# Attention with shared latents on one core: latents stationary in P.V, probabilities normalised before they are split

## The chip, the core and the metric

One Trainium2 chip, one of its cores. The kernel is one program of five engine queues: TensorE (PE), VectorE (DVE), ScalarE (ACT), GpSimd (POOL), and SyncE (SP), which issues all DMAs. The metric is the time of one execution on the device in microseconds, lower is better; the median of three executions is given.

## What is computed

A transformer layer on 2 x 1024 tokens of width 512. First latent attention with 32 heads, then a gated feed-forward part with whole-number weights. Only the attention is touched:

```python
q = (rms_norm(x @ wq_a.T) @ wq_b.T).reshape(b, s, 32, 128 + 64)      # rope on the last 64
kv = x @ wkv_a.T                                                     # 64 latents + 64 rope
kv_up = (rms_norm(kv_c) @ wkv_b.T).reshape(b, s, 32, 128 + 128)      # k_nope, v per head
scores = (q_nope @ k_nope.T + q_pe @ k_pe.T) * scale                 # causal mask
probs = softmax(scores)
out = (probs @ v) @ wo.T
x = x + layernorm(out)
```

The kernel never forms keys and values of a head. It folds the key weights into the query weights (`weff`), so that scores are queries against the 64 latents and 64 rotated columns that all heads share, and it folds each head's value weights with its part of `wo` (`m_fold`), so that P.V is probabilities times the 64 shared latents. Numbers that need more than one rounding are carried as a high and a low half.

## The kernel before

There are 64 heads (2 sequences x 32). A head has 8 query tiles of 128 tokens; tile j has (j + 1) x 128 keys, since later ones are masked. A pair of neighbouring tiles in the order `TILES` always has 9 key tiles together. For each tile i the steps are:

- PE `scores` (L1021): three matmuls for every stretch of up to 512 keys, into one of four PSUM slots `s_ps`, taken in turn. It waits for `split_low` of tile i - 4, the last reader of the slot.
- DVE `minimum` (L1453): adds the mask and takes the row minimum (scores are negated).
- ACT `exponential` (L1230), in place; then ACT `split_high` (L1238), probabilities times 2^15 rounded to f16; then DVE `split_low` (L1466), the rest, in f16.
- For two tiles together SP `turn_probs` (L822): one DMA transpose of both halves, from `pk` into `pt`.
- PE `values` (L1035): 18 matmuls, probabilities stationary, latents moving. The latents hold a high half, a low half and two columns of ones, 130 columns; the ones give the row sums.
- DVE `invert_sums` (L1462) reads the sums, ACT `outputs_norm` (L1247) scales the outputs into SBUF, twice a pair; POOL `outputs_add` (L1649) adds the two halves for four tiles.
- For two heads together PE `outputs_turn` (L1044) transposes four 128x128 tiles into the one bank `x_ps`, ACT `outputs_high` (L1256) and DVE `outputs_low` (L1473) split them.

Beside this runs `queries` for the next head (five matmuls into `x_ps`, ACT copy, two DMAs that swap rows, four POOL steps of rotation, POOL splits them into high and low), `fold_values` in the first 32 heads (into `x_ps` also), and for each group of four heads `output` (six matmuls a tile, `x_ps`) and `output_add` (DVE, L1489). Two PSUM banks are left beside the six of `s_ps`: `o_ps` and `x_ps`.

The order on every engine is fixed when the program is built. `attention_order` gives each step a place on a common scale, one unit to a tile (`at`, `then`), sorts them, and each engine runs its own steps in that order. Before, a step's distance from its tile is one number for all tiles. A place says only who comes before whom in one queue; when a step runs is decided by the semaphores it waits for.

Of the kernel before, what the change touches and what calls it, by code (L numbers as in the profile page):

```python
# [11 lines left out]
P = 128  # L12
# [23 lines left out]
NX, NA, NPK, NPT, NON = 4, 3, 3, 5, 8  # L36

SLOTS = (1, 2, 2, 1)
# [4 lines left out]
AFTER_SCORES = dict(minimum=0.8, exponential=1.24, split_high=2.06, split_low=2.28)  # L43
TURN_PROBS = 2.44
VALUES = 8.04
AFTER_VALUES = dict(invert_sums=1.21, outputs_norm=1.63, outputs_add=0.63)
TURN_STEPS = (6.26, 6.09)
AFTER_TURN = dict(outputs_high=0.27, outputs_low=0.95)
Q_STEPS = (0.84, 2.95)
AFTER_QUERIES = dict(queries_raw=0.13, queries_swap=0.31, queries_turn=0.13)  # L50
O_STEPS = (3.4, 6.23)
AFTER_OUTPUT = dict(output_add=1.26, output_store=1.5)
FOLD_STEP = 1.03
AFTER_FOLD = dict(fold_high=0.17, fold_low=1.03, fold_store=1.5)
# [24 lines left out]

LATW = P + 2  # L80
# [5 lines left out]
TILES = (3, 4, 6, 1, 2, 5, 7, 0)  # L86
# [15 lines left out]

def halves(j):

    width = (j + 1) * P
    return [(c, min(CW, width - c)) for c in range(0, width, CW)]
# [31 lines left out]
class Signals:  # L138


    def __init__(self, new):
# [67 lines left out]
def ot_count(n, c):  # L209

    return n // 2 * 2 + c + 1

# [57 lines left out]
class Memory:  # L270
    def __init__(self, whole, nc):
# [3 lines left out]
        with ExitStack() as attn:  # L275
# [5 lines left out]
            self.lat2 = sb(attn, "lat2", [P, NT, LATW], F16)  # L281
            sb(attn, "spare", [P, 2048 - NT * LATW // 2])
# [52 lines left out]
    def attention(self, ctx, sb, pb):  # L335
        self.m_in = sb(ctx, "m_in", [P, 2, GK, 2, DM], F32R)
        self.nbias = sb(ctx, "nbias", [P, 4])
        self.rinv = sb(ctx, "rinv", [P, NON])
        self.pk = sb(ctx, "pk", [P, NPK, 2 * PAIR, P], F16)
        self.pt = sb(ctx, "pt", [P, NPT, 2 * PAIR, P], F16)  # L340
        self.o_norm = sb(ctx, "o_norm", [P, NON, P])
        self.o_pair = sb(ctx, "o_pair", [P, 2, 4, P])
# [110 lines left out]
def attention_order(end):  # L453
# [1317 lines left out]
```

## Time and profile before

| | us |
|---|---|
| median of 3 runs | 1653.72 |
| lowest, highest | 1653.41, 1660.02 |
| profiled execution | 1654.97 |
| its span, first to last instruction | 1653.2 |

The profile is one execution. Its page gives busy times of the engines, the span in 40 slices, the DMA queues, the chain of work that ended last, and the costliest groups of instructions. Attention fills about the stretch from 100 to 1230 us, and its first 32 heads are those that also fold.

### The profile page before, as it was taken

The numbers are of one execution on the slowest core, as the hardware profiler recorded it, in microseconds if no ns is written. First come the engines' busy times: TensorE is split into PE (matmuls) and PEld (weight loads), VectorE is DVE, ScalarE is ACT, GpSimd is POOL, SyncE is SP. The second block draws the span as 40 slices with busy tenths as digits, with TensorE's granted clock in tenths as the row PEclk, the third lists the DMA queues.
The fourth block names the chain that finished last, engine by engine and source line by source line (L and its number), as shares of the span: only waits on it lengthen the run. The fifth ranks groups of instructions, "written<-read, shape, count | busy, mean of one in ns | idle before, by whom it ended". The sixth has DMA issues, their size and how long they took to land.

```text
span 1653.2 us, 30456 instructions
## 1 busy us (share of the span) xinstructions
PE 1552.6 (94%) x10720; PEld 1291.8 (78%) x10720; DVE 1113.6 (67%) x2509; ACT 1109.4 (67%) x2203; POOL 954.6 (58%) x913
## 2 busy tenths in 40 slices
PE   6878999999999999999999999999987999999997
PEld 5766788788887788787888888888865778888875
DVE  6767777778887777876788778887775342323344
ACT  5677888787887787877888878887765553212134
POOL 2656767677776777677776778777723221111124
PEclk9899999999999999999999999999999999999999
DMA  8659999999999999999999999998997200101022
GB/s 285 232 146 204 186 205 189 198 182 197 214 176 200 186 202 198 192 197 193 177 195 184 177 191 188 184 192 172 186 203 269 83 27 18 59 1 40 1 77 102
DMA packets 661096, 268.85 MB, mean 163 GB/s; under 512 B 608432, under 2 KB 619184, under 8 KB 658768
## 3 DMA queue, kind: packets, MB, share of 16 engines
q1 hardware_dynamic: 660944, 266.90, 75.3%
q8 instruction: 86, 1.41, 0.3%
q14 instruction: 66, 0.54, 0.1%
HBM read 69.70 MB, written 29.36 MB: 60 GB/s over the span
## 4 chain that ended last, share of the span: by engine, by line
PE 68%; DVE 8%; POOL 8%; ACT 7%; DMA 5%; issue 3%; SPq 2%; POOLq 0%; ACTq 0%; DVEq 0%
PE s_ps L1021 17%; PE x_ps L121 15%; PE f_ps L121 13%; PE o_ps L1035 12%; PE fd_ps L121 6%; DMA qs<-q_raw 2%; POOL qf L1625 2%; POOL q_low L1632 2%; POOL qs L1622 2%; SPq L822 2%; PE x_ps L1044 1%; DMA pt<-pk 1%; DMA weff_in<-weff 1%; ACT pk L1238 1%; ACT ot_high L1256 1%
## 5 line engine op out<-in xcount | busy, mean ns | idle before, releaser
L1466 DVE SCALAR_TENSOR_TENSOR pk<-s_ps,pk 128x512 f16<-128x512 f32 (+7 forms) x512 | 386.1, 754 | 116.1 <-ACT pk L1238 114.2
L1230 ACT ACTIVATE s_ps<-s_ps,nbias 128x512 f32<-128x512 f32 (+7 forms) x512 | 366.2, 715 | 94.1 <-DVE nbias L1453 85.2
L1453 DVE CUSTOM_DVE_ANT_0 s_ps<-s_ps,far_sb 128x512 f32<-128x512 f32 (+7 forms) x512 | 387.9, 758 | 47.9 <-PE s_ps L1021 47.7
L1238 ACT ACTIVATE pk<-s_ps 128x512 f16<-128x512 f32 (+7 forms) x512 | 336.1, 657 | 18.8 <-DMA pt<-pk 12.9
L1035 PE MATMUL o_ps<-lat,pt 128*128 128x130 f16 x4608 | 311.3, 221 | 9.2 <-ACT o_norm L1247 9.1
L1035 PEld LDWEIGHTS o_ps<-lat,pt 128*128 128x128 f16 x4608 | 267.2, 98 | 42.9 <-issue 35.7
L1021 PE MATMUL s_ps<-k_high,q_high 128*128 128x512 f32 (+3 forms) x768 | 278.9, 363 | 15.7 <-POOL q_low L1632 10.7
L1622 POOL TENSOR_TENSOR qs<-qs,sin_q 64x512 f32<-64x512 f32 x128 | 164.6, 1286 | 204.3 <-DMA qs<-q_raw 197.1
L1021 PE MATMUL s_ps<-k_low,q_high 128*128 128x512 f32 (+3 forms) x768 | 258.1, 348 | 0.0
L1663 POOL TENSOR_TENSOR mid_low<-mid,mid_high 128x512 fp32r<-128x512 f32 (+1 forms) x44 | 56.9, 1293 | 300.3 <-ACT mid_high L1327 300.3
L1021 PE MATMUL s_ps<-k_high,q_low 128*128 128x512 f32 (+3 forms) x768 | 225.8, 348 | 0.0
L1021 PEld LDWEIGHTS s_ps<-k_high,q_high 128*128 128x128 f32 x768 | 145.5, 189 | 45.5 <-POOL q_low L1632 18.0
L1619 POOL TENSOR_TENSOR qf<-q_raw,cos_q 128x512 f32<-128x512 f32 x128 | 164.1, 1282 | 28.0 <-ACT q_raw L1220 11.8
L1632 POOL TENSOR_TENSOR q_low<-qf,q_high 128x512 fp32r<-128x512 f32 x128 | 164.6, 1286 | 10.2
L1625 POOL TENSOR_TENSOR qf<-qf,qs 64x512 f32<-64x512 f32 x128 | 164.3, 1284 | 10.0
L1247 ACT ACTIVATE o_norm<-o_ps,rinv 128x128 f32<-128x128 f32 x512 | 161.4, 376 | 8.3 <-DVE rinv L1462 6.3
L121 PE MATMUL x_ps<-m_in,ot_high 128*128 128x512 f32 x492 | 163.5, 413 | 2.5 <-DVE ot_low L1473 1.5
L1021 PEld LDWEIGHTS s_ps<-k_low,q_high 128*128 128x128 f32 x768 | 146.1, 190 | 21.4
L1551 DVE TENSOR_TENSOR mid<-f_ps,gate 128x512 f32<-128x512 f32 (+1 forms) x44 | 30.4, 690 | 179.1 <-PE f_ps L121 140.6
L1021 PEld LDWEIGHTS s_ps<-k_high,q_low 128*128 128x128 f32 x768 | 135.9, 190 | 8.7
L121 PE MATMUL f_ps<-ft_high,w_high 128*128 128x512 f32 (+1 forms) x352 | 138.3, 393 | 1.4 <-DVE ft_low L1527 1.4
L121 PE MATMUL f_ps<-ft_high,w_low 128*128 128x512 f32 (+1 forms) x352 | 138.2, 393 | 0.0
(142 smaller groups left out, 2608.0 us busy)
## 6 DMA issues: line engine op xcount, KB each, us to landing
weff_in<-weff SPq DMA_DIRECT2D x64, 256.0 KB, 3.2
qs<-q_raw SPq DMA_DIRECT2D x256, 64.0 KB, 2.2
weff<-weff_sb SPq DMA_DIRECT2D x8, 1024.0 KB, 5.3
wo_sb<-wo SPq DMA_DIRECT2D x16, 512.0 KB, 4.6
m_fold<-m_in SPq DMA_DIRECT2D x8, 1024.0 KB, 6.7
m_in<-m_fold SPq DMA_DIRECT2D x8, 1024.0 KB, 6.3
xin<-x SPq DMA_DIRECT2D x16, 256.0 KB, 4.8
wqn_sb<-wqn SPq DMA_DIRECT2D x8, 512.0 KB, 6.9
```

What stands on the lines that cost most here:

```text
L121: ins = e.matmul(out, stationary, moving, start=start and n == 0, stop=stop and n == len(pairs) - 1)
L1021: ins = e.matmul(s[:, c:c + width], queries[:, r, q], side[:, keys], start=queries is M.q_high and side is M.k_high, stop=queries is M.q_low)
L1035: ins = e.matmul(M.o_ps[:, i % 2, :], M.pt[:, u % NPT, m, :], M.lat2[:, b * JT + (m - blocks[0]) // 2, :], start=m == blocks[0], stop=m == ...
L1230: e.activation(M.scores_of(i), M.scores_of(i), ACT.Exp, bias=M.nbias[:, i % 4:i % 4 + 1], scale=-1.0).then_inc(S.exp)
L1238: e.activation(M.halves_of(i)[:, :, 0, :], M.tiles_of(i), ACT.Copy, scale=P_SCALE).then_inc(S.p_high)
L1247: ins = e.activation(M.o_norm[:, r, :], M.o_ps[:, side, 0:P], ACT.Copy, scale=M.rinv[:, r:r + 1])
L1453: e.tensor_tensor_reduce(out=s, in0=s, in1=M.far_sb[:, SEQ - width:SEQ], scale=1.0, scalar=3e38, op0=ALU.add, op1=ALU.min, accum_out=M.nbi ...
L1466: e.scalar_tensor_tensor(out=M.halves_of(i)[:, :, 1, :], in0=M.tiles_of(i), scalar=P_SCALE, in1=M.halves_of(i)[:, :, 0, :], op0=ALU.mult, ...
L1619: e.tensor_tensor(M.qf[:, c, :], M.raw[:, c, :], M.cos_q[:, col], ALU.mult).then_inc(S.q_cos)
L1622: e.tensor_tensor(M.qs[KVL:P, c, :], M.qs[KVL:P, c, :], M.sin_q[KVL:P, col], ALU.mult).then_inc(S.q_sin)
L1625: e.tensor_tensor(M.qf[KVL:P, c, :], M.qf[KVL:P, c, :], M.qs[KVL:P, c, :], ALU.add).then_inc(S.q_turned)
L1632: e.tensor_tensor(M.q_low[:, n % 2, col], M.qf[:, c, :], f32(M.q_high[:, n % 2, col]), ALU.subtract).then_inc(S.q_split)
```

## The change

`values` is turned round: the latents of a key tile are the stationary operand, and the probabilities of both tiles of a pair move through together (256 columns) as long as both have that key tile, then those of the wider tile alone (128). The output comes out with latents on the partitions and tokens along the row: four tiles fill one `o_ps` bank. The columns of ones are gone. The row sums come from the exponential's accumulator instead, are inverted by pair before the split, and both split steps multiply by the inverse. `outputs_norm`, `outputs_add` and `outputs_turn` go. In their place ACT `outputs_side` copies 64 partitions of `o_ps` (the low latents' half) for four tiles, DVE `outputs_sum` adds the other 64; `outputs_high` reads the sum from SBUF, and `outputs_low` moves to POOL.

```diff
-SLOTS = (1, 2, 2, 1)
+SLOTS = (1, 2, 1, 2)
-TILES = (3, 4, 6, 1, 2, 5, 7, 0)
+TILES = (3, 4, 2, 5, 0, 7, 1, 6)
+def first_col(j):
+    return P if (j + 1) * P % CW == P and j else 0
...
     def values(u):
-        if u:
-            w.wait_ge(S.o_norm, u)
-                ins = e.matmul(M.o_ps[:, i % 2, :], M.pt[:, u % NPT, m, :],
-                               M.lat2[:, b * JT + (m - blocks[0]) // 2, :], start=m == blocks[0],
-                               stop=m == blocks[-1])
+        if u % 2 == 0 and k:
+            w.wait_ge(S.o_sum, k)
+                if t < min(tiles):
+                    out, probs = both, pt[:, m:m + step + 1:step, :]
+                else:
+                    wide = tiles.index(max(tiles))
+                    out, probs = both[:, wide, :], pt[:, m + wide * step, :]
+                ins = e.matmul(out, M.lat2[:, b * JT + t, :], probs, start=m == 0,
+                               stop=m == 2 * max(tiles) - 1)
...
-                     scale=-1.0).then_inc(S.exp)
+                     scale=-1.0, accum_out=M.sums[:, i % NSUM:i % NSUM + 1]).then_inc(S.exp)
     def split_high(i):
-        w.wait_ge(S.exp, i + 1)
+        w.wait_ge(S.rinv, u + 1)
-        e.activation(M.halves_of(i)[:, :, 0, :], M.tiles_of(i), ACT.Copy, scale=P_SCALE
+        e.activation(M.halves_of(i)[:, :, 0, :], M.tiles_of(i), ACT.Copy,
+                     scale=M.rinv[:, r:r + 1]).then_inc(S.p_high)
+    def outputs_side(k):
+        w.wait_ge(S.pv, 2 * k + 2)
+        e.activation(M.o_side[side, k % 2, :], M.o_ps[other, :], ACT.Copy, scale=O_SCALE
+                     ).then_inc(S.o_side)
...
     def invert_sums(u):
-        w.wait_ge(S.pv, u + 1)
-        e.reciprocal(M.rinv[:, r:r + 2], M.o_ps[:, :, P]).then_inc(S.rinv)
+        w.wait_ge(S.exp, 2 * u + 2)
+        e.tensor_scalar(M.sums[:, r:r + 2], M.sums[:, r:r + 2], 1.0 / P_SCALE, None, ALU.mult
+                        ).then_inc(S.scaled)
+        w.wait_ge(S.scaled, u + 1)
+        e.reciprocal(M.rinv[:, r:r + 2], M.sums[:, r:r + 2]).then_inc(S.rinv)
+    def outputs_sum(k):
+        w.wait_ge(S.o_side, k + 1)
+        e.scalar_tensor_tensor(out=M.o_sum[side, c, :], in0=M.o_ps[side, :], scalar=O_SCALE,
+                               in1=M.o_side[side, c, :], op0=ALU.mult, op1=ALU.add
+                               ).then_inc(S.o_sum)
```

The single distances are replaced by tables with one number for each of the 8 places in a head (or 4 pairs, 2 halves, 8 output tiles), of which this is a part:

```diff
-AFTER_SCORES = dict(minimum=0.8, exponential=1.24, split_high=2.06, split_low=2.28)
+TILE_STEPS = dict(
+    minimum=(1.16, 0.51, -0.07, 0.1, 1.54, 1.04, 0.4, 0.9),
+    split_low=(2.51, 2.58, 3.87, 3.4, 4.13, 3.14, 3.42, 2.63),
```

On PE, around the values of one pair of tiles in the middle of the attention, before (`s_ps` are scores, `x_ps` queries or outputs):

```order
L1021 MATMUL s_ps<-k_high,q_low 128x512
L1021 MATMUL s_ps<-k_high,q_low 128x128
L1035 MATMUL o_ps<-lat,pt 128x130 x18
L1021 MATMUL s_ps<-k_high,q_high 128x512
L1021 MATMUL s_ps<-k_low,q_high 128x512
```

And now, from the end of one head into the next:

```order
L161 MATMUL x_ps<-qb_both,weff_in 128x512 x2
L1078 MATMUL o_ps<-pt,lat 128x256 x4
L1078 MATMUL o_ps<-pt,lat 128x128 x10
L1055 MATMUL s_ps<-k_high,q_high 128x512
L1055 MATMUL s_ps<-k_low,q_high 128x512
L1055 MATMUL s_ps<-k_high,q_low 128x512
L1055 MATMUL s_ps<-k_high,q_high 128x384
L1055 MATMUL s_ps<-k_low,q_high 128x384
L1055 MATMUL s_ps<-k_high,q_high 128x256
L1055 MATMUL s_ps<-k_low,q_high 128x256
L1055 MATMUL s_ps<-k_high,q_low 128x384
L1055 MATMUL s_ps<-k_high,q_low 128x256
```

Between the values of a head's last pair and those of the next head's first pair now stand the scores of the 512- and 640-key tiles, and the 640 keys are cut 384 + 256.

On DVE, the stretch from the minimum of a 1024-key tile on, before (the instruction called ISA is the minimum; the second of its lines reads its accumulator):

```order
L1453 ISA s_ps,nbias<-s_ps,far_sb 128x1024 [waits s_mm]
L1453 ISA nbias 128x1
L1466 SCALAR_TENSOR_TENSOR pk<-s_ps,pk 128x6x128 [waits p_high]
L1489 TENSOR_TENSOR acc<-x_ps,acc 128x512 [waits sum_more,op_mm]
L1453 ISA s_ps,nbias<-s_ps,far_sb 128x128 [waits s_mm]
L1453 ISA nbias 128x1
L1462 RECIPROCAL rinv<-o_ps 128x2 [waits o_normed,pv_mm]
L1466 SCALAR_TENSOR_TENSOR pk<-s_ps,pk 128x8x128 [waits p_high]
```

And now from the minimum of the 896-key tile (scores slot 3) to its split:

```order
L1488 ISA s_ps,nbias<-s_ps,far_sb 128x896 [waits s_mm]
L1488 ISA nbias 128x1
L1506 SCALAR_TENSOR_TENSOR pk<-s_ps,rinv,pk 128x128 [waits p_high]
L1506 SCALAR_TENSOR_TENSOR pk<-s_ps,rinv,pk 128x8x128 [waits p_high]
L1498 TENSOR_SCALAR sums<-sums 128x2 [waits p_low,exp_done]
L1501 RECIPROCAL rinv<-sums 128x2 [waits sums_scaled]
L1516 SCALAR_TENSOR_TENSOR o_sum<-o_ps,o_side 64x512 [waits ot_low,o_side]
L1488 ISA s_ps,nbias<-s_ps,far_sb 128x512 [waits s_mm]
L1488 ISA nbias 128x1
L1506 SCALAR_TENSOR_TENSOR pk<-s_ps,rinv,pk 128x2x128 [waits p_high]
L1488 ISA s_ps,nbias<-s_ps,far_sb 128x640 [waits s_mm]
L1488 ISA nbias 128x1
```

The line after these is the split_low of the 896-key tile. Before, two to four other steps stood between a tile's minimum and its split_low; now there are seven, and the inversion that both splits of a pair wait for stands among them.

## Rows read from the trace of the kernel before

**Rows 1.** The page: busy us and instructions; the chain's shares by engine.
```profile
PE 1552.6 (94%) x10720; PEld 1291.8 (78%) x10720; DVE 1113.6 (67%) x2509; ACT 1109.4 (67%) x2203; POOL 954.6 (58%) x913
...
PE 68%; DVE 8%; POOL 8%; ACT 7%; DMA 5%; issue 3%; SPq 2%; POOLq 0%; ACTq 0%; DVEq 0%
```

**Rows 2.** Busy time by stretch: four heads with folds, four without.
```profile
core 0: us, PE busy (x) PEld busy (x) DVE busy (x) ACT busy (x) POOL busy (x), PEclk, DMA share, GB/s
596.60:666.50 69.90, 68.94 (x545) 57.74 (x544) 56.18 (x127) 56.20 (x111) 51.89 (x49) 1.00 0.94 192
1049.60:1116.90 67.30, 66.74 (x536) 57.03 (x535) 55.25 (x126) 55.23 (x108) 50.06 (x47) 1.00 0.98 184
```

**Rows 3.** The same view for the minimum alone (L1453), 1000 us.
```profile
200.00:1200.00 1000.00, 370.25 (x908) 0.99 0.97 190
```

**Rows 4.** Timeline of DVE: start, us, instruction; each head's first minimum.
```profile
630.02 0.69 DVE L1453 CUSTOM_DVE_ANT_0 s_ps<-s_ps,far_sb 128x512 f32<-128x512 f32 x1
...
647.08 0.69 DVE L1453 CUSTOM_DVE_ANT_0 s_ps<-s_ps,far_sb 128x512 f32<-128x512 f32 x1
...
1049.63 0.69 DVE L1453 CUSTOM_DVE_ANT_0 s_ps<-s_ps,far_sb 128x512 f32<-128x512 f32 x1
...
1065.68 0.69 DVE L1453 CUSTOM_DVE_ANT_0 s_ps<-s_ps,far_sb 128x512 f32<-128x512 f32 x1
...
1083.31 0.69 DVE L1453 CUSTOM_DVE_ANT_0 s_ps<-s_ps,far_sb 128x512 f32<-128x512 f32 x1
...
1099.26 0.69 DVE L1453 CUSTOM_DVE_ANT_0 s_ps<-s_ps,far_sb 128x512 f32<-128x512 f32 x1
...
1116.86 0.69 DVE L1453 CUSTOM_DVE_ANT_0 s_ps<-s_ps,far_sb 128x512 f32<-128x512 f32 x1
```

**Rows 5.** The chain in order of time: start, us, what.
```profile
1064.48 1.15 PE x_ps L121 x5
...
1066.60 1.04 PE o_ps L1035 x18
1067.64 0.46 PE x_ps L1044 x4
...
1070.93 0.36 PE s_ps L1021 x3
```

**Rows 6.** Groups of ACT by shape: count, busy us, mean ns, idle before.
```profile
L1183 ACT ACTIVATION_READ_ACCUMULATOR squares<-a_ps 128x1 f32 x16 | 3.7, 229 | 0.0
...
L1247 ACT ACTIVATE o_norm<-o_ps,rinv 128x128 f32<-128x128 f32 x454 | 143.2, 376 | 1.2 <-DVE rinv L1462 1.2
...
L1256 ACT ACTIVATE ot_high<-x_ps 128x512 fp32r<-128x512 f32 x56 | 33.5, 598 | 48.1 <-PE x_ps L1044 48.1
...
L1238 ACT ACTIVATE pk<-s_ps 128x128 f16<-128x128 f32 x57 | 15.5, 271 | 0.0
```

**Rows 7.** Groups of DVE by shape, the same columns.
```profile
L1473 DVE SCALAR_TENSOR_TENSOR ot_low<-x_ps,ot_high 128x512 fp32r<-128x512 f32 x56 | 38.8, 692 | 47.1 <-ACT ot_high L1256 47.1
...
L1480 DVE SCALAR_TENSOR_TENSOR m_in<-x_ps,kv_weight,m_in 128x512 fp32r<-128x512 f32 x14 | 10.5, 751 | 11.1 <-ACT m_in L1266 11.1
...
L1407 DVE TENSOR_SCALAR kvw_row<-kvw_row 128x64 f32<-128x64 f32 x1 | 0.2, 185 | 0.0
```

**Rows 8.** A group of POOL by shape, the same columns.
```profile
L1632 POOL TENSOR_TENSOR q_low<-qf,q_high 128x512 fp32r<-128x512 f32 x114 | 146.7, 1287 | 9.1
```

**Rows 9.** Waits from 200 to 1200 us: total, times, longest.
```profile
DVE pk L1466 <- ACT pk L1238: 96.7, 136, 2.4
...
PEld x_ps L121 <- DVE ot_low L1473: 28.8, 56, 0.6
```

**Rows 10.** The transposes on the SP queue: shortest, median, longest ns.
```profile
L822 SPq DMA_TRANSPOSE pt<-pk x228: 2445/2924/5971, 199.6 to 1199.2; - x114
```

**Rows 11.** Timeline of DVE: an 896-wide tile's minimum and split_low.
```profile
599.63 1.10 DVE L1453 CUSTOM_DVE_ANT_0 s_ps<-s_ps,far_sb 128x896 f32<-128x896 f32 x1 [0.25 <-PE s_ps L1021]
...
603.25 1.09 DVE L1466 SCALAR_TENSOR_TENSOR pk<-s_ps,pk 128x896 f16<-128x896 f32 x1 [0.87 <-ACT pk L1238]
```

More of the change, by code:

```diff
@@ L35 @@
 STEPS = NH // FH
-NX, NA, NPK, NPT, NON = 4, 3, 3, 5, 8
-SLOTS = (1, 2, 2, 1)
+NX, NA, NPK, NPT, NSUM = 4, 3, 3, 5, 8
+SLOTS = (1, 2, 1, 2)
 NS = len(SLOTS)
 CW = 512
-AFTER_SCORES = dict(minimum=0.8, exponential=1.24, split_high=2.06, split_low=2.28)
[L44 to L54, printed above, removed]
+TILE_STEPS = dict(
+    minimum=(1.16, 0.51, -0.07, 0.1, 1.54, 1.04, 0.4, 0.9),
+    exponential=(1.79, 0.81, 1.19, 1.56, 2.21, 1.95, 1.33, 1.35),
+    split_high=(2.08, 3.11, 3.6, 3.63, 4.08, 3.22, 2.9, 2.61),
+    split_low=(2.51, 2.58, 3.87, 3.4, 4.13, 3.14, 3.42, 2.63),
+)
+PAIR_STEPS = dict(
+    invert_sums=(0.68, 1.66, 2.72, 1.96),
+    turn_probs=(2.46, 0.53, 0.74, 3.44),
+    values=(8.22, 8.55, 9.99, 8.33),
+)
+CHUNK_STEPS = dict(
+    outputs_side=(9.27, 9.8),
+    outputs_sum=(9.58, 10.12),
+)
+ROW_STEPS = dict(
+    outputs_high=(11.81, 10.67),
+    outputs_low=(9.56, 5.71),
+)
+QUERY_STEPS = dict(
+    queries=(-1.0, 1.98),
+    queries_raw=(0.24, 1.97),
+    queries_swap=(-3.62, 2.57),
+    queries_turn=(-1.12, 3.41),
+)
+OUTPUT_STEPS = dict(
+    output=(11.63, 13.51, 20.11, 21.96, 28.99, 29.4, 36.86, 37.54),
+    output_add=(13.51, 14.89, 21.22, 22.91, 29.49, 31.06, 36.92, 38.84),
+)
+FOLD_STEPS = dict(
+    fold_values=(0.12, -0.38),
+    fold_high=(1.12, 1.62),
+    fold_low=(1.5, 1.14),
+)
+QUERIES_LOAD, OUTPUT_LOAD, FOLD_STORE = 3.11, 35.67, 0.86
+VALUES_LOAD = (0.45, 6.26)
+OUTPUT_STORE = (15.76, 15.78, 21.46, 22.58, 30.49, 30.5, 37.68, 39.28, 1.5)
+LAST_OUTPUT = dict(output=(0.0,), output_add=(1.26,))
 END_STEP, END_EVERY = 16.49, 3.75
@@ L100, in f32 @@
     return ap.bitcast(F32)
+def first_col(j):
+    return P if (j + 1) * P % CW == P and j else 0
 def halves(j):
-    width = (j + 1) * P
-    return [(c, min(CW, width - c)) for c in range(0, width, CW)]
+    first, width = first_col(j), (j + 1) * P
+    ends = sorted({0, width} | {c - first for c in range(CW, first + width, CW)})
+    return [(c, end - c) for c, end in zip(ends, ends[1:])]
 def three(a_high, a_low, b_high, b_low):
@@ L1358, in scalar_program @@
              weights_high=weights_high, queries_raw=queries_raw, latents_over=latents_over,
[L1359 to L1360 removed]
+             exponential=exponential, split_high=split_high, outputs_side=outputs_side, outputs_high=outputs_high,
+             fold_high=fold_high, output_add=output_add,
              feed_forward_begins=feed_forward_begins, deviations=deviations,
```

177 lines of the change are left out of this document (77 added, 100 removed).

## The prediction

> **What bounds the kernel now.** I began with the busy times and the chain of work that ended last [rows 1]: TensorE is busy for 94% of the span and carries 68% of the chain; DVE, POOL, ACT and DMA carry 5 to 8% each. The change touches the attention stage only, so I read that next, in stretches of four heads: 69.9 us where two of the four also fold a weight pair, 67.3 us where none does, with PE busy for 99% in both, DVE and ACT for 55 to 56 us, POOL for 50 to 52, and the granted clock at 1.00, which is the 2.4 GHz level [rows 2]. So PE sets the pace, but nothing else is idle for more than a quarter of it, and the DMA engines are marked 0.94 and 0.98 busy.
>
> The starts of the first minimum of each head give the pitch [rows 4]. The heads follow one another after 16.05, 17.63, 15.95 and 17.60 us. The short ones are heads in which no outputs are turned on PE, the long ones have both turns of a pair of heads. A head that folds and turns nothing takes 17.06, so a fold costs 1.1 us. In regular running eight heads take 69.9 + 67.3 = 137.2 us, 17.15 each. Over 1000 us there are 908 records of the minimum, two to an instruction and eight instructions to a head: 56.75 heads, 17.62 us each [rows 3]. The 0.47 us between is irregular delay (late queries, late weights), 30 us over 64 heads.
>
> **What goes from PE.** Four transposes take 0.46 us on the chain [rows 5], and there are 64 such groups: 29 us. The rest of the difference between long and short heads, 17.6 - 16.0 - 2 x 0.46 = 0.7 us a pair of heads, is what the turn makes others wait: the one bank x_ps stays taken until ACT and then DVE have read it, and the next matmuls into it wait (28.8 us in 1000 on the weight loads [rows 9], part of it beside running matmuls). That is another 22 us. After the change no PE step stands between the values and the output projection, so every head should be a short head: this is the gain, 1.6 us in every second head. The folds still pay 1.1.
>
> **Values turned round.** Before, 72 matmuls a head with 130 columns, 18 in 1.04 us, 58 ns each [rows 5]: 4.18 us. Now 20 with 256 columns and 32 with 128. No f16 matmul with 256 columns is in the trace. From below it is 0.107, one column a cycle at 2.4 GHz; from above the 0.12 us of a 256-column scores matmul (0.36 for three [rows 5]). A 512-column one takes 0.23 (five in 1.15 [rows 5]), 0.45 ns a column, as the 130-column ones do, and at that rate 256 columns take 0.115, which I use. The 128-column ones I put at 57 ns. Sum 20 x 0.115 + 32 x 0.057 = 4.12, a gain of 0.05 a head, with ends 3.96 and 4.25. The scores of the tile with 640 keys are now cut 384 + 256 and not 512 + 128. Three of 0.175 and three of 0.12 make 0.89, three of 0.23 and three of 0.06 to 0.11 made 0.87 to 1.02: 0.04 gained. A bare head is then 16.0 - 0.05 - 0.04 = 15.9 us.
>
> The Trainium skill (TensorE: Matmul & The Clock Gate, Back-to-back issue gap) gives N / 2.4 + 2.5 ns for an isolated warm matmul, 55.8 ns for 128 columns and 109.2 for 256; the trace's 58 ns for 130 columns lies 1 ns above it. By the page the new values would cost 3.97 us and the sum would be 10 us lower. The same section holds that a stream of loads and matmuls pays some 81 ns at 128 columns; the trace speaks against that.
>
> **What comes onto the other engines, per head.** DVE: two outputs_sum, 64x512 from PSUM, 0.69 each by the nearest row of that length [rows 7]; one outputs_low leaves for POOL, 0.69; four small multiplies before the reciprocals, at most the 0.185 of a 128x64 one [rows 7]; and eight split_low whose scale is now a column of numbers. The same operation on 128x512 took 692 ns with a constant and 751 with a column [rows 7], so 0.06 each. Together 1.38 - 0.69 + 0.74 + 0.48 = +1.9 us on 13.8 [rows 2]: 15.7. ACT: the eight outputs_norm of 0.376 go (3.0), two outputs_side of 0.60 come; eight split_high also get a column for a scale, 0.376 against 0.271 for the same shape [rows 6], +0.84; eight exponentials now read out their sum, 0.229 each, if fully exposed 1.8, and at least 0.7 as I judge by its overlap with the main instruction. Together between -0.2 and +0.9 on 13.8. POOL: two additions go, one outputs_low of 1.29 comes [rows 8]; no change. On PE these engines' time costs nothing so long as it is covered. A head has 15.9 us of PE work, and DVE has 15.7: the cover is nearly used up, and this is where the forecast can fail.
>
> **The new waits.** Normalising first means that split_high waits for invert_sums, which waits for the exponentials of both tiles of a pair. A score slot is therefore held longer. Before, from the start of a 896-wide minimum to the end of its split_low were 4.7 us (599.63 to 604.34 [rows 11]). In the new order DVE does between the same two points split_low 128 and 1024, a sum inversion, outputs_sum, minimum 512, split_low 256, minimum 640: with the widths' times about 6.7 us. The slot of the 768 and 896 tiles is used twice in a head, and its two holds with their scores come to 7.8 + 8.0 us, about the PE time of a head. I followed one head through the new orders. With t = 0 at the end of the 896-wide scores, PE does queries (1.15) and values (1.03), then scores 512 and 640, and stands before the next values at 3.8. That step needs the one o_ps bank back. ACT can't start outputs_side before the exponential of 896 has run behind a 1.1 us minimum, at 2.65; the copy ends at 3.25, DVE's sum at 3.95: PE waits 0.2. The scores of 768 wait for split_low of 896, about 0.1. The rest have 0.1 to 1.2 us to spare. So 0.3 us of new stall a head, with a lower end of 0 and an upper end set by DVE, below. Queued behind these waits on PE are scores and queries of the next tiles, on which all the others feed.
>
> **DMA and POOL.** The same 256 transposes stay. One occupies the SP queue for 2.9 us [rows 10], 11.7 a head before swaps and loads. Queries (both halves) come one to two steps earlier against the scores that use them, which gives POOL more room; the m_in load now stands ahead of a swap that has 7 us to spare. I keep the irregular 0.47 us a head as it is. Prologue, the last group's output steps and the feed-forward part are the same; the small memset costs nothing.
>
> **The sum.** Eight regular heads: 8 x (15.9 + 0.3) + 2 x 1.1 = 131.8 us against 137.2, 5.4 less; eight such sets give 43 us. The profiled execution took 1654.97 us, so 1612; it lies 1.2 us above the median of the runs, and I forecast **1611 us**. With the stall between 0.1 and 0.6 and the values' ends it is 1598 to 1632.
>
> **Rivals.** *The cover holds entirely:* no stall, values at the lower end. 15.7 us a head, 32 us more gained at most: 1585 to 1598, middle 1592. DVE's load speaks against it. *The queue of DMAs takes over:* if a head's transfers can't go below 16.5 us, eight heads take 132 plus what folds and the 1 MB loads add, 134.5, and 22 us are gained: 1633. For it speaks the share of 0.94 to 0.98 [rows 2]; against it, that PE waits for no transposed probabilities in the trace. The Trainium skill (DMA: Bandwidth & Descriptors, Latency and other measured facts) puts a DMA transpose at 261 GB/s, by which the four of a head would need some 9 us and the queue would have room; the measured 2.9 us of issue each is more than that. *Stalls eat it:* 1.0 us a head of waiting on DVE and ACT, and it is 1655 again. *The slot ring decides, slower:* DVE idled 3.0 us a head before, most of it in-order waiting for ACT (96.7 us in 1000 before split_low alone [rows 9]). If 2.0 of these 3.0 us stay, the period is 15.7 + 2.0 = 17.7 us against 16.8, and the kernel takes 64 x 0.9 = 58 us longer: 1712; with 1.5 us it is 1680. It decides from 1.1 us on, that is, if the ten hand-overs around the 768/896 slot cost 0.1 us more each than I counted. Ahead of it speaks how little spare time my trace left; against, that a busier DVE waits less, since what it waits for is done by then. *The change doesn't do what it says:* the transposes are gone from PE's order, so only the steps could fail, by waiting; that is the case above.
>
> **Numbers.** About 0.5% either way is what a measurement of this kernel tells from no change, 8 us. Chances: forecast band 1598 to 1632 0.50, cover holds 0.13, DMA or part stalls 1632 to 1645 0.12, no change 0.10, slower 0.15. Faster 0.75, same 0.10, slower 0.15. The range of 8 in 10 leaves out half of the fully covered case and most of the slow one: 1589 to 1665.
>
> **What would show it.** Right: heads of equal length, 16.2 us (17.3 with a fold), no long and short; 64x512 sums on DVE near 0.69; values 4.1 us a head; DVE busy above 93% of attention. PE's new idle should stand before the values after a head's fourth pair, released by outputs_sum, and before 768-wide scores, released by split_low. Wrong: idle of more than 1 us a head before scores (ring), PE waiting for pt or q_low (DMA), or a 256-column matmul above 0.12 us.

## The result and the profile after

| | before | after |
|---|---|---|
| median | 1653.57 us | 1674.24 us |
| lowest, highest | 1651.72, 1660.02 | 1673.51, 1674.89 |
| profiled execution, its span | 1654.97, 1653.2 | 1674.89, 1673.1 |

Each kernel was executed four times. The ratio is 1.012, 95% interval 1.009 to 1.015: the change made the kernel slower by 1.2%. I had forecast 1611 us, and the time lies outside my range.

The page of the changed kernel, to hold against [rows 1]: busy us and instructions of each engine, then the shares of the chain that ended last, by engine and by line.

```profile
PE 1534.1 (92%) x9184; PEld 1226.9 (73%) x9184; DVE 1292.7 (77%) x2829; ACT 1153.4 (69%) x2331; POOL 941.5 (56%) x848
...
DVE 40%; PE 33%; ACT 16%; issue 8%; DMA 1%; POOL 1%; SPq 0%; DVEq 0%; POOLq 0%
```

PE lost 1536 instructions and 18.5 us of busy time, as it should. DVE gained 179 us where I had counted 1.9 us a head, 122 in all, and it leads the chain, where PE stood with 68%.

The same two kinds of stretch as in [rows 2], four heads with folds and four without (us, PE busy, PEld busy, DVE busy, ACT busy, POOL busy, granted clock, DMA share, GB/s):

```profile
644.26:717.55 73.29, 68.52 (x450) 54.46 (x449) 68.22 (x147) 59.29 (x119) 51.04 (x44) 1.00 0.91 195
1049.07:1118.90 69.83, 66.46 (x440) 53.37 (x440) 65.92 (x144) 57.84 (x117) 51.09 (x44) 1.00 0.80 182
```

They were 69.9 and 67.3 us long. The granted clock is 1.00, so the clock isn't it. PE is no longer full (95%), and DVE is busy for 94%: 65.92 / 4 = 16.5 us a head, where I had 15.7.

The starts of the heads' first minima, as in [rows 4]:

```profile
1049.07 0.70 DVE L1488 CUSTOM_DVE_ANT_0 s_ps<-s_ps,far_sb 128x512 f32<-128x512 f32 x1
...
1067.09 0.68 DVE L1488 CUSTOM_DVE_ANT_0 s_ps<-s_ps,far_sb 128x512 f32<-128x512 f32 x1
...
1084.26 0.70 DVE L1488 CUSTOM_DVE_ANT_0 s_ps<-s_ps,far_sb 128x512 f32<-128x512 f32 x1
...
1102.27 0.68 DVE L1488 CUSTOM_DVE_ANT_0 s_ps<-s_ps,far_sb 128x512 f32<-128x512 f32 x1
```

18.0, 17.2 and 18.0 us. The long heads are longer than the old long ones (17.6), and the short heads of 16 us are gone.

Now the groups of DVE by shape (count, busy us, mean ns, idle before), from 200 to 1200 us:

```profile
L1498 DVE TENSOR_SCALAR sums<-sums 128x2 f32<-128x2 f32 x224 | 110.1, 491 | 13.6 <-ACT s_ps L1265 12.7
...
L1501 DVE RECIPROCAL rinv<-sums 128x2 f32<-128x2 f32 x224 | 37.1, 166 | 7.7
...
L1516 DVE SCALAR_TENSOR_TENSOR o_sum<-o_ps,o_side 64x512 f32<-64x512 f32 x112 | 76.8, 686 | 9.4 <-ACT o_side L1283 6.9
```

The sum of outputs takes the 0.69 us that I gave it. But the small multiply, two numbers a partition, takes 491 ns on average, and the reciprocal of the same two numbers right behind it takes 166. The view of that one line gives shortest, median and longest ns:

```profile
L1498 DVE TENSOR_SCALAR sums<-sums x224: 150/361/1273, 200.6 to 1196.7; 128x2 f32<-128x2 f32 x112
```

An instruction whose time goes from 0.15 to 1.27 us isn't computing for that long; it is held. By what, the timelines of POOL and of DVE over the same 3 us show:

```profile
656.78 1.29 POOL L1674 TENSOR_TENSOR q_low<-qf,q_high 128x512 fp32r<-128x512 f32 x1
658.22 1.28 POOL L1688 TENSOR_TENSOR ot_low<-o_sum,ot_high 128x512 fp32r<-128x512 f32 x1
```

```profile
656.27 0.69 DVE L1532 TENSOR_TENSOR acc<-x_ps,acc 128x512 f32<-128x512 f32 x1
656.88 1.22 DVE L1498 TENSOR_SCALAR sums<-sums 128x2 f32<-128x2 f32 x1
658.13 0.17 DVE L1501 RECIPROCAL rinv<-sums 128x2 f32<-128x2 f32 x1
658.22 1.08 DVE L1488 CUSTOM_DVE_ANT_0 s_ps<-s_ps,far_sb 128x896 f32<-128x896 f32 x1
```

POOL's instruction runs from 656.78 to 658.07. The multiply starts at 656.88 and ends at 658.10, right behind it. I compared all multiplies of the kernel with POOL's timeline: in 189 of 256 a POOL instruction was running at the start, and they took 599 ns on average; the 67 others took 168 ns. Of the 189, 174 took over 0.2 us, and each of these ended 21 to 29 ns behind the end of that POOL instruction. The reciprocals take 166 ns whether POOL is running or not. Nor is any other DVE instruction of the attention stage held: each shape of minimum, split_low, outputs_sum and output_add has the same mean, to within 20 ns, whether POOL was running at its start or not.

What the wait costs is in the waits, 200 to 1200 us (total, times, longest):

```profile
ACT pk L1273 <- DVE rinv L1501: 104.8, 137, 1.9
...
PEld s_ps L1055 <- DVE pk L1506: 37.3, 81, 1.2
PEld x_ps L161 <- DVE acc L1532: 33.0, 48, 1.7
...
PE s_ps L1055 <- DVE pk L1506: 19.9, 44, 0.9
PE o_ps L1078 <- DVE o_sum L1516: 17.8, 43, 1.3
...
PE x_ps L161 <- DVE acc L1532: 13.7, 23, 1.2
```

ACT stands before its splits for the inverse, and PE stands for everything that DVE does behind the multiply: split_low, output_add, outputs_sum.

### The profile page after: what moved, and what is told of

It is laid out like the page before. It is cut to its first block, busy times and chain, and to the rows that moved or that the text cites. A ratio compares the mean times of both kernels' runs of the same rounds, so it can differ in the third digit from the quotient of the medians.

```text
span 1673.1 us, 27504 instructions
## 1 busy us (share of the span) xinstructions
PE 1534.1 (92%) x9184; PEld 1226.9 (73%) x9184; DVE 1292.7 (77%) x2829; ACT 1153.4 (69%) x2331; POOL 941.5 (56%) x848
## 4 chain that ended last, share of the span: by engine, by line
DVE 40%; PE 33%; ACT 16%; issue 8%; DMA 1%; POOL 1%; SPq 0%; DVEq 0%; POOLq 0%
PE f_ps L161 13%; DVE s_ps L1488 11%; DVE pk L1506 9%; ACT pk L1273 6%; PE fd_ps L161 6%; DVE sums L1498 5%; PE x_ps L161 5%; PE s_ps L1055 5%; DVE o_sum L1516 4%; DVE acc L1532 3%; ACT s_ps L1265 3%; PE o_ps L1078 2%; ACT o_side L1283 2%; ACT q_raw L1255 2%; DVE rinv L1501 1%
## 5 line engine op out<-in xcount | busy, mean ns | idle before, releaser
L1273 ACT ACTIVATE pk<-s_ps,rinv 128x512 f16<-128x512 f32 (+7 forms) x512 | 365.3, 737 | 120.8 <-DVE rinv L1501 118.2
L1506 DVE SCALAR_TENSOR_TENSOR pk<-s_ps,rinv,pk 128x512 f16<-128x512 f32 (+7 forms) x512 | 412.5, 812 | 21.1 <-ACT pk L1273 20.9
L1055 PE MATMUL s_ps<-k_high,q_high 128*128 128x512 f32 (+3 forms) x768 | 289.2, 377 | 37.5 <-DVE pk L1506 36.0
L1078 PE MATMUL o_ps<-pt,lat 128*128 128x128 f16 (+1 forms) x3328 | 299.0, 241 | 22.3 <-DVE o_sum L1516 22.3
L1078 PEld LDWEIGHTS o_ps<-pt,lat 128*128 128x128 f16 x3328 | 241.6, 98 | 80.2 <-issue 60.3
L161 PE MATMUL x_ps<-m_in,ot_high 128*128 128x512 f32 x492 | 163.7, 414 | 16.1 <-DVE acc L1532 15.7
L1688 POOL TENSOR_TENSOR ot_low<-o_sum,ot_high 128x512 fp32r<-128x512 f32 x64 | 82.4, 1287 | 143.3 <-ACT ot_high L1291 138.9
L1055 PEld LDWEIGHTS s_ps<-k_low,q_high 128*128 128x128 f32 x768 | 146.2, 190 | 15.7
L161 PE MATMUL f_ps<-ft_low,w_high 128*128 128x512 f32 (+1 forms) x352 | 138.8, 394 | 0.0
```

The costliest lines, as they stand in the source:

```text
L161: ins = e.matmul(out, stationary, moving, start=start and n == 0, stop=stop and n == len(pairs) - 1)
L1055: ins = e.matmul(s[:, c:c + width], queries[:, r, q], side[:, keys], start=queries is M.q_high and side is M.k_high, stop=queries is M.q_low)
L1078: ins = e.matmul(out, M.lat2[:, b * JT + t, :], probs, start=m == 0, stop=m == 2 * max(tiles) - 1)
L1273: e.activation(M.halves_of(i)[:, :, 0, :], M.tiles_of(i), ACT.Copy, scale=M.rinv[:, r:r + 1]).then_inc(S.p_high)
L1506: e.scalar_tensor_tensor(out=M.halves_of(i)[:, :, 1, :], in0=M.tiles_of(i), scalar=M.rinv[:, r:r + 1], in1=M.halves_of(i)[:, :, 0, :], op0 ...
```

## The theories, and the first four kernels

**Theory W:** the multiply is held by the POOL instruction that is running, and that is what separates 1674 from my forecast. **Theory R** is the rival that I had priced beforehand: normalising first makes the hold of a score slot too long (the sum inversion stands between a tile's exponential and its split), and the multiply is only one small part of that chain. All four kernels start from the changed one; the kernel before, on the same chip, took 1652.94 us.

**The multiply left out.** Its factor goes into the scale of the outputs, so the whole computation is done.

```diff
-O_SCALE = 1.0 / (P_SCALE * L_SCALE)
+O_SCALE = 1.0 / L_SCALE
...
-        e.tensor_scalar(M.sums[:, r:r + 2], M.sums[:, r:r + 2], 1.0 / P_SCALE, None, ALU.mult
-                        ).then_inc(S.scaled)
-        w.wait_ge(S.scaled, u + 1)
```

> The small multiply of the row sums by 2^-15 on DVE is left out, and the probabilities aren't scaled by 2^15 before they are split. In the changed kernel this multiply takes 491 ns in the mean and up to 1273, where 168 would be expected. Theory W (the multiply is held until a running POOL instruction is over, and this is what lengthens the heads): the multiplies' 256 x 0.49 = 126 us of DVE time go, and the head falls from 17.9 us to 16.3 to 16.6; 1590 to 1615 us. Theory R (normalising before the split makes the slot ring too long whatever the multiply costs): the ring gets only the 0.17 us back that the multiply should cost, 1660 to 1670 us.

Measured: 1616.43 us, ratio to before 0.978 (0.976 to 0.981).

**A reciprocal in its place**, of the same two numbers, in place, with the same hand-over. The number of steps and of waits stays; the probabilities are then not normalised.

```diff
-        e.tensor_scalar(M.sums[:, r:r + 2], M.sums[:, r:r + 2], 1.0 / P_SCALE, None, ALU.mult
-                        ).then_inc(S.scaled)
+        e.reciprocal(M.sums[:, r:r + 2], M.sums[:, r:r + 2]).then_inc(S.scaled)
```

> The multiply is replaced by a second reciprocal of the same two columns, so DVE has the same number of small instructions in the same places; the row sums come out inverted twice, so that the probabilities are not normalised. The one existing small reciprocal took 166 ns whether or not POOL was busy. Theory W: the second one takes 0.17 us too, 82 us of held DVE time go; 1600 to 1630 us. Theory R: within 8 us of the changed kernel, 1666 to 1680 us.

Measured: 1619.91 us, 0.980 (0.977 to 0.983). The view of the line, shortest, median and longest ns:

```profile
L1498 DVE RECIPROCAL sums<-sums x232: 152/166/168, 203.9 to 1183.2; 128x2 f32<-128x2 f32 x116
```

**The multiply moved to ACT**, behind the pair's second exponential.

```diff
+    def scale_sums(u):
+        r = 2 * u % NSUM
+        w.wait_ge(S.exp, 2 * u + 2)
+        e.activation(M.sums[:, r:r + 2], M.sums[:, r:r + 2], ACT.Copy, scale=1.0 / P_SCALE
+                     ).then_inc(S.scaled)
```

> The multiply moves to ACT, behind the exponential of the second tile of a pair. Everything is still computed. Theory W: the holding goes, ACT gets some 0.2 us four times a head, DVE loses 0.17 us four times; 1600 to 1635 us. Theory R: ACT's additional wait for its own exponential makes the ring longer, 1670 to 1700 us.

Measured: 1634.14 us, 0.989 (0.986 to 0.991). The step takes ACT 204 ns, and DVE now stands 53.8 us in 1000 before the reciprocal.

**The splits freed from the inverse.** Both take the constant 2^15 and wait for their own exponential; the multiply and the reciprocal stay on DVE, unused, so the probabilities are not normalised.

```diff
-        w.wait_ge(S.rinv, u + 1)
+        w.wait_ge(S.exp, i + 1)
...
-                     scale=M.rinv[:, r:r + 1]).then_inc(S.p_high)
+                     scale=P_SCALE).then_inc(S.p_high)
...
-                               scalar=M.rinv[:, r:r + 1], in1=M.halves_of(i)[:, :, 0, :], op0=ALU.mult, op1=ALU.subtract
+                               scalar=P_SCALE, in1=M.halves_of(i)[:, :, 0, :], op0=ALU.mult, op1=ALU.subtract
```

> Both splits use the constant 2^15 again and split_high waits for its own exponential alone; the row sums are still scaled and inverted on DVE in the same places, but nobody uses them, so the probabilities are not normalised. The multiply is still held by POOL. Theory W: DVE keeps nearly its whole load (0.5 us a head less for the column scale) and the held multiply in its queue; 1650 to 1670 us. Theory R: the ring is short again and every head is near 16.2 us; 1605 to 1625 us.

Measured: 1650.42 us, 0.998 (0.997 to 1.000).

W's range holds in three of the four, for two of them within 1 us of its edge, and it misses the first by 1.4 us. R's numbers are 25 to 46 us away from all of them. The second shows that it isn't the step: a reciprocal with the same place, the same operands and the same two waits costs 3.5 us over none at all, and the multiply costs 54 more than the reciprocal (1674.24 - 1619.91). The fourth shows that a held multiply that nobody waits for still costs 44 us (1606.81 with the multiply left out as well, in the section after the next), as DVE's own queue stands behind it. With the splits waiting, leaving the multiply out gave 58 us (1674.24 - 1616.43). So about 14 us of the hold come about only through the waiting splits, which is where the two theories meet.

## How the hold works

Two kernels on the mechanism, and three on its condition. Where it says nothing else, they start from the changed kernel, and all compute everything. Before: 1654.91 us for the next three, 1653.07 for the one-column multiply, 1652.22 for the last.

**POOL's instructions in halves.** Each of the five of queries_turn and outputs_low becomes two of 256 columns:

```diff
+        def halves(op, sem):
+            for h in (lo, hi):
+                ins = op(h, slice(cc + h.start, cc + h.stop))
+            ins.then_inc(sem)
...
-        e.tensor_tensor(M.qf[:, c, :], M.raw[:, c, :], M.cos_q[:, col], ALU.mult).then_inc(S.q_cos)
+        halves(lambda h, col: e.tensor_tensor(M.qf[:, c, h], M.raw[:, c, h], M.cos_q[:, col], ALU.mult),
+               S.q_cos)
```

> The changed kernel with every POOL instruction of the attention stage (rotation and split of the queries, outputs_low) written as two of 256 columns instead of one of 512; nothing is left out. Theory W (the multiply is held until the POOL instruction that is running at its start has ended): the hold can last no longer than one such half, some 0.65 us, the multiply's mean duration falls from 0.49 to 0.28 to 0.38 us and the kernel to 1635 to 1660 us, although POOL has as much work and more instructions. Rival (POOL being busy slows or blocks the multiply by its share of time, whatever the length of an instruction): mean 0.49 us, 1670 to 1680 us.

**Two multiplies**, by 2^-7 and by 2^-8.

```diff
-        e.tensor_scalar(M.sums[:, r:r + 2], M.sums[:, r:r + 2], 1.0 / P_SCALE, None, ALU.mult
-                        ).then_inc(S.scaled)
-        w.wait_ge(S.scaled, u + 1)
+        for half in range(2):
+            e.tensor_scalar(M.sums[:, r:r + 2], M.sums[:, r:r + 2], 2.0 ** (-7 - half), None,
+                            ALU.mult).then_inc(S.scaled)
+            w.wait_ge(S.scaled, 2 * u + half + 1)
```

> The changed kernel with the small multiply done in two steps, by 2^-7 and by 2^-8; nothing is left out. Theory W: the second one follows while POOL has gone on to its next instruction, so it is often held as well; the two take 0.7 to 1.0 us together and the kernel 1690 to 1730 us. Rival R (a multiply costs only a step of 0.17 us and its hand-over in a chain of waits; the reciprocal in its place cost 3.5 us over none at all): 1676 to 1682 us.

**A product of two tiles** in place of the product with a constant. The tile `inv_p` holds 2^-15 in two columns and is filled once, before the first multiply.

```diff
+        if u == 0:
+            e.memset(M.inv_p[:, :], 1.0 / P_SCALE).then_inc(S.scaled)
...
-        e.tensor_scalar(M.sums[:, r:r + 2], M.sums[:, r:r + 2], 1.0 / P_SCALE, None, ALU.mult
+        e.tensor_tensor(M.sums[:, r:r + 2], M.sums[:, r:r + 2], M.inv_p[:, :], ALU.mult
```

> The changed kernel with the small multiply written as TENSOR_TENSOR, the sums times a tile of two columns of 2^-15; nothing is left out. If only an instruction that can use both pairs of DVE's ports for one tensor is held (TENSOR_SCALAR from SBUF to SBUF), it takes 0.17 to 0.2 us each time and the kernel 1616 to 1626 us. If a DVE instruction with two inputs in SBUF is held in the same way by a POOL instruction that reads SBUF, its mean is 0.4 to 0.5 us and the kernel 1660 to 1680 us. In between (slowed, not held): 0.2 to 0.3 us and 1626 to 1650 us.

**One column each.**

```diff
-        e.tensor_scalar(M.sums[:, r:r + 2], M.sums[:, r:r + 2], 1.0 / P_SCALE, None, ALU.mult
-                        ).then_inc(S.scaled)
+        e.tensor_scalar(M.sums[:, r:r + 1], M.sums[:, r:r + 1], 1.0 / P_SCALE, None, ALU.mult)
+        e.tensor_scalar(M.sums[:, r + 1:r + 2], M.sums[:, r + 1:r + 2], 1.0 / P_SCALE, None,
+                        ALU.mult).then_inc(S.scaled)
```

> The changed kernel with the small multiply written as two of one column each; nothing is left out. If an instruction of a single element a partition can't be spread over both pairs of ports, it isn't held: 0.16 us each, 1620 to 1632 us. If the form alone decides (TENSOR_SCALAR from SBUF to SBUF, whatever its size), the first of the two is held as the one of two columns is, and now and then the second as well: 1675 to 1700 us.

**One column each, as a product of two tiles.** The edit is shown against the product of two tiles above.

```diff
-        e.tensor_tensor(M.sums[:, r:r + 2], M.sums[:, r:r + 2], M.inv_p[:, :], ALU.mult
-                        ).then_inc(S.scaled)
+        e.tensor_tensor(M.sums[:, r:r + 1], M.sums[:, r:r + 1], M.inv_p[:, 0:1], ALU.mult)
+        e.tensor_tensor(M.sums[:, r + 1:r + 2], M.sums[:, r + 1:r + 2], M.inv_p[:, 1:2], ALU.mult
+                        ).then_inc(S.scaled)
```

> The small multiply as two TENSOR_TENSOR of one column each, the sums times a tile of 2^-15; nothing is left out. Theory P (what counts is which pair of ports an instruction needs: TENSOR_SCALAR needs the one shared with POOL only where it can halve its elements, a second input from SBUF needs it always): these are held as the one of two columns was, the first to a mean of some 0.5 us and the second now and then, 1675 to 1700 us. Rival (an instruction of one element is too small to be held, whatever it reads): 0.16 us each, 1620 to 1632 us.

Measured:

| kernel | us | ratio to before, interval | mean ns |
|---|---|---|---|
| changed kernel | 1674.24 | 1.012 (1.009 to 1.015) | 491 |
| POOL in halves | 1656.68 | 1.001 (1.000 to 1.003) | 409 |
| two multiplies | 1710.79 | 1.034 (1.032 to 1.036) | 330 (x2) |
| product of two tiles | 1680.38 | 1.016 (1.013 to 1.018) | 493 |
| one column each | 1623.32 | 0.981 (0.979 to 0.984) | 151 and 144 |
| one column, two tiles | 1692.10 | 1.023 (1.021 to 1.026) | 481 and 176 |

The view of the line in each of the five, in that order (shortest, median, longest ns):

```profile
L1498 DVE TENSOR_SCALAR sums<-sums x228: 157/404/753, 201.6 to 1196.0; 128x2 f32<-128x2 f32 x114
```

```profile
L1499 DVE TENSOR_SCALAR sums<-sums x434: 157/170/1297, 202.3 to 1199.1; 128x2 f32<-128x2 f32 x145
```

```profile
L1502 DVE TENSOR_TENSOR sums<-sums,inv_p x223: 140/358/1222, 202.4 to 1198.4; 128x2 f32<-128x2 f32 x112
```

```profile
L1498 DVE TENSOR_SCALAR sums<-sums x232: 140/153/156, 204.1 to 1187.1; 128x1 f32<-128x1 f32 x116
```

```profile
L1502 DVE TENSOR_TENSOR sums<-sums,inv_p x220: 143/331/1266, 203.5 to 1195.7; 128x1 f32<-128x1 f32 x110
```

What follows. With POOL in halves of 0.74 us the longest hold is 0.75 instead of 1.27: a held instruction waits for the end of the POOL instruction that is running, and gets in before the next one. The mean fell less than I had expected (409 ns, not 280 to 380), since the halves take POOL 0.74 each and not half of 1.28, so POOL is busy for 821 us in 1000 instead of 715, and 218 of the 256 multiplies began beside a POOL instruction; the kernel still gained 18 us with more work on POOL. Of two multiplies the second is seldom held: it follows right behind POOL's end, and 17 of 256 took over 0.2 us where 138 of the first did. Together they take 0.66 us, under the 0.7 to 1.0 that I had expected. The kernel is 37 us slower; 256 times the added 0.17 us of DVE time is 43, so here the time fits a plain step in DVE's full queue as well, and only the spread (170 at the median, 1297 at the longest) speaks for the hold. The product of two tiles took 1680.38 us, 0.4 above the range for a held one, with its mean inside (0.49).

The last three show the condition. The product with a constant is held with two columns and never with one. The product of two tiles is held with two columns and with one. So a small size alone doesn't protect an instruction; what it reads counts too. The Trainium skill has this (SBUF — State Buffer, Who interferes with whom): DVE and GpSimd share one pair of SBUF ports as an exclusive lock; a tensor_scalar from SBUF to SBUF can enter a mode that takes that pair too, and then whoever issues first blocks the other for the whole instruction; an instruction with two inputs in SBUF contends with a GpSimd instruction that reads SBUF, since its second input comes through the shared read interface. The Trainium skill (VectorE: DVE Perf Modes, Mode 2×_2P) asks for that mode an outermost non-unit dimension that is even, or odd and equal in source and destination; one column has no such dimension. The runs agree: 1273 ns and 1222 ns at the longest for the two forms with two columns, 156 for the constant with one, 1266 for two tiles with one, and 168 at most for the reciprocal, which the Trainium skill doesn't list among the operations that take the pair.

The ports themselves are in no trace; the runs show only which forms are held. The other instructions of DVE in the attention stage, a column used as a scale not counted, have at most one input in SBUF, and they aren't held. The other direction shows in the kernel before: a POOL instruction of 128x64 at 78.82 us, 0.10 us behind the start of a DVE TENSOR_SCALAR of 128x512 from SBUF to SBUF, took 0.63 us; 16 of this form have a median of 0.32. The rule was there to be applied before I forecast.

## What is left without the hold

**No multiply, and the splits freed too**: the first and the fourth kernel together; the probabilities are not normalised.

> The small multiply is left out, and both splits take the constant 2^15 and wait only for their own exponential (the sums are still inverted, but nothing uses them, so the probabilities are not normalised: this leaves that part out). Theory A: once the multiply is gone, what still lies above my forecast is the longer hold of the score slots that comes with normalising first. Then it gives 1590 to 1605 us, with PE's waits before scores on DVE's split_low (some 30 us in 1000 with the multiply left out alone) down to 10 or less. Rival B: the slots are no limit any more, and PE waits for the one bank o_ps: then 1612 to 1617 us, as with the multiply left out alone, and the waits before values on outputs_sum stay at 20 in 1000.

Measured: 1606.81 us, 0.971 (0.969 to 0.973). It lies between what the two named. PE's waits before values stayed (22.0 us in 1000, 20.4 in the kernel without the multiply), those before scores fell little (6.8 for 8.7 on the matmuls, 14.3 for 22.7 on the loads). So normalising first, with its longer chain and its scales in a column, costs 9.6 us by the times; by the ratios it is 12, as the two kernels ran on different chips. With the hold in place the same edit gave 24 us (1674.24 - 1650.42). That is the real size of what Theory R was about.

**outputs_side ahead of the exponential of the 896-key tile**, from the kernel without the multiply:

```diff
-    outputs_side=(9.27, 9.8),
-    outputs_sum=(9.58, 10.12),
+    outputs_side=(9.27, 9.3),
+    outputs_sum=(9.58, 9.9),
```

> The kernel without the multiply (its factor 2^-15 is taken into the scale of the outputs; nothing is left out), and in every head outputs_side for the last two pairs stands ahead of the exponential of the 896-key tile on ACT, and outputs_sum ahead of the inversion on DVE. Theory A, as the prediction had it: PE stands before a head's first values because outputs_side comes behind that exponential; 0.84 us of idle stood there in a head of the run without the multiply, 0.6 of it can go, and at worst the exponential ends 0.6 us later: 1590 to 1608 us. Rival B: the exponential moved back delays the inversion, the split and with them the slots, and takes the gain back: 1612 to 1625 us.

Measured: 1623.78 us, 0.982 (0.979 to 0.985), 7 slower than without the edit; Rival B. The waits of PE, 200 to 1200 us, first without the edit, then with it:

```profile
PE o_ps L1078 <- DVE o_sum L1513: 20.4, 44, 2.8
PE s_ps L1055 <- DVE pk L1503: 8.7, 12, 1.0
```

```profile
PE s_ps L1055 <- DVE pk L1503: 20.7, 39, 1.0
PE x_ps L161 <- DVE m_in L1520: 6.6, 7, 0.9
```

The stall before the values is gone but for one wait of 2.3 us, as I had argued, and PE waits before the scores instead: before 768-wide ones, 0.48 us at 1043.6. A bare head stays at 16.6 us, so nothing is gained. I put this down to the later exponential, which makes the inverse and the slot late; no run separates that. What makes the kernel slower is the head with folds, 20.1 us for 19.2: DVE stands 2.02 us for ACT before fold_low where it stood 1.28.

**fold_low behind the next head's minimum**, from the kernel without the multiply; it was ahead of it in every second pair.

```diff
-    fold_low=(1.5, 1.14),
+    fold_low=(1.5, 1.17),
```

> The kernel without the multiply (its factor is taken into the scale of the outputs; nothing is left out), with fold_low of every second pair behind the next head's minimum of 512 columns on DVE and no longer ahead of it (its place 1.17 for 1.14). Theory A: in the run without the multiply DVE stood 1.28 us for ACT at that fold_low, with the minimum queued behind it; 0.6 to 1.3 us in each of the 15 heads with two folds or in 8 of them as the trace has it go, 5 to 10 us together: 1606 to 1612 us. Rival B: that head is held up by PE's bank x_ps, which comes free no sooner: 1615 to 1618 us.

Measured: 1609.93 us, 0.975 (0.972 to 0.977), 6.5 less than without the edit; Theory A. DVE's timeline without the edit shows the wait with the minimum behind it:

```profile
631.05 0.75 DVE L1520 SCALAR_TENSOR_TENSOR m_in<-x_ps,kv_weight,m_in 128x512 fp32r<-128x512 f32 x1 [1.28 <-ACT m_in L1301]
631.72 0.69 DVE L1488 CUSTOM_DVE_ANT_0 s_ps<-s_ps,far_sb 128x512 f32<-128x512 f32 x1
```

And with it:

```profile
627.60 0.70 DVE L1488 CUSTOM_DVE_ANT_0 s_ps<-s_ps,far_sb 128x512 f32<-128x512 f32 x1
628.85 0.75 DVE L1520 SCALAR_TENSOR_TENSOR m_in<-x_ps,kv_weight,m_in 128x512 fp32r<-128x512 f32 x1 [0.45 <-ACT m_in L1301]
```

Four heads with folds had pitches of 16.5, 16.6, 16.6 and 19.2 us; now 16.6, 16.6, 17.3 and 17.8. This is the fastest that computes everything: 42 us under the kernel before, 64 under the changed one.

## Why the prediction was wrong, step by step

**The step that failed is one term of DVE's sum:** "four small multiplies before the reciprocals, at most the 0.185 of a 128x64 one [rows 7]". They took 0.49 each, 1.97 us a head for my 0.74. I took one instruction of the prologue, when POOL left it alone, for an upper end. The rest of that sum held: with the multiply left out DVE was busy for 58.98 / 4 = 14.7 us a bare head, and my sum without the term is 15.0.

The trace of the kernel before already had the sign, 16 instructions of the same operation from SBUF to SBUF in the prologue, all of one shape, with columns for their scalars:

```profile
L1392 DVE TENSOR_SCALAR xn<-xin,mv,rstd x16: 545/547/1318, 12.1 to 78.7; 128x512 f32<-128x512 f32 x16
```

Seven of the 16 took 627 to 1318 ns, and each of the seven ended 0.28 us behind the end of a POOL instruction that had run beside it. One of them, with that POOL instruction:

```profile
68.69 1.32 DVE L1392 TENSOR_SCALAR xn<-xin,mv,rstd 128x512 f32<-128x512 f32 x1
```

```profile
68.44 1.28 POOL L1610 TENSOR_TENSOR weff_sb<-wqp_sb,weff_sb 128x512 fp32r<-128x512 f32 x1
```

With the term as I had it (the reciprocal in its place at 0.163, or two of one column at 0.151 and 0.144), the kernel takes 1620 and 1623 us, inside my band of 1598 to 1632. The hold alone is 54 us, more than the whole gain of 43 that I had forecast.

**The rival that came true in its outcome was right for another reason.** "The slot ring decides, slower", to which I gave 0.15, has DVE at 15.7 us of work and 2.0 of waits. DVE waited little (of 69.83 us for four heads it was busy for 65.92); its instructions were longer. What I named as its mechanism is worth about 10 us without the hold. One of my signs of being right misled for the same reason: DVE busy above 93% came true in the slower kernel (94%), as a held instruction counts as busy, and not in the kernel without the multiply (89%).

**The gain of the turns** was right in kind: in the kernel without the multiply all bare heads are alike. The timeline of DVE there:

```profile
1015.92 0.68 DVE L1488 CUSTOM_DVE_ANT_0 s_ps<-s_ps,far_sb 128x512 f32<-128x512 f32 x1
...
1032.56 0.70 DVE L1488 CUSTOM_DVE_ANT_0 s_ps<-s_ps,far_sb 128x512 f32<-128x512 f32 x1
...
1049.19 0.68 DVE L1488 CUSTOM_DVE_ANT_0 s_ps<-s_ps,far_sb 128x512 f32<-128x512 f32 x1
```

That is 16.6 us each; I had 16.2. **Stalls** of PE there are 0.50 us a head (20.4 + 8.7 in 1000, 58 heads), not 0.3, at the two places that I had named: before values behind outputs_sum 0.35, and before scores behind split_low 0.15. Taken off the 16.6, they leave 16.1 of PE's work in a bare head, not 15.9.

**The values** were right. The chain of the kernel without the multiply has the four pairs of a head (start, us, instructions):

```profile
609.64 1.01 PE o_ps L1078 x14
...
613.49 1.00 PE o_ps L1078 x10
...
617.43 1.01 PE o_ps L1078 x12
...
623.36 1.02 PE o_ps L1078 x16
```

Together 4.04, for my 4.12. Of the ten instructions eight have 256 columns, of the sixteen two: 8a + 2b = 1.00 and 2a + 14b = 1.02 give a = 0.111 and b = 0.057; I had 0.115 and 0.057.

**The folds** cost 1.3 each in the kernel without the multiply, not 1.1. With that, eight regular heads take 135.5 us (69.0 and 66.5) for my 131.8; this alone would have put the kernel at 1641, not 1616. **The irregular delay** of 0.47 us a head, which I kept, made up for it: that the kernel without the multiply lands near my 1611 is luck in part. The changed kernel has 895 records of the minimum in 1000 us, 55.9 heads, 17.88 us each, and its regular heads take (73.29 + 69.83) / 8 = 17.89: nothing irregular is left. That is 30 us, of both signs to the forecast: eight regular heads went from 137.2 to 143.1, which is 47 us slower, and 30 came back; the difference is 17, measured 21. Before, PE's matmuls waited 9.5 us in 1000 for q_low and 4.1 for weights, after for neither. I put this down to the earlier queries, but no run tests it.

**ACT and POOL** were as counted: split_high with a column takes 367 ns for 271 [rows 6], reading out the sum 198 for 229, outputs_side 592, outputs_low on POOL 1287.

**DMA** wasn't the limit: its share fell to 0.80 in a stretch without folds, and is 0.84 in such a stretch of the kernel without the multiply.

**Two sums of the range** don't come out as I wrote them. The cover's 0.5 us a head, 32 us, leads from 1611 to 1579 at the lowest and not 1585. The ends of the stall and of the values, added up, give 1588 to 1638 and not 1598 to 1632. The measured time lies outside either.

So the chances were misplaced in one respect. I gave 0.15 to slower, with a price worked out from waits, and none to an operation that is held, though the trace of before showed that operation held seven times. That is 1611 forecast, and 1609.93 in a kernel that differs from the changed one by that instruction and one fold step, though by errors that cancel.

## What to carry to other kernels

Before adding a small DVE instruction to a loop in which POOL is busy for half the time, ask where its operands are: the product of two SBUF tiles, with one column or two, and the product with a constant from SBUF to SBUF, with two columns, waited for up to a whole POOL instruction here. Fold the factor into an existing scale (58 us here), or write the instruction in a form that isn't held (one column at a time with a constant: 51 us for an edit of one statement). In a profile, the sign is a group with a mean far above its shortest; look at shortest, median and longest of the line, and hold one of its long instructions against POOL's timeline.

## What the runs showed of the hardware

- A 128x2 multiply on DVE took 0.15 to 1.27 us, by what POOL was doing; 189 of 256 began beside a running POOL instruction and took 0.60 us on average, for the 0.17 that the others take.
- The hold ends with the POOL instruction that runs, about 25 ns behind it, and DVE gets in before POOL's next one.
- A 128x512 TENSOR_SCALAR from SBUF to SBUF took 0.55 us alone and up to 1.32 beside POOL, in the kernel before.
- A product of two SBUF tiles with one column is held (1266 ns at the longest), a product with a constant with one column isn't (156). A reciprocal of two columns isn't either (168).
- Cutting POOL's instructions of 128x512 in two costs 0.74 + 0.74 us for 1.28, and still made the kernel 18 us faster.
